# Attention: the queries' turn moved from a head's first step to its third, and their copy from ScalarE to VectorE

## What is computed

```python
Q, K, V = proj(Wq, bq), proj(Wk, bk), proj(Wv, bv)      # 64 heads x 2048 x 32
query_norms = jnp.linalg.norm(Q, axis=2)
_, top_idx = jax.lax.top_k(query_norms, top_u)          # top_u = 409
Q_sel = jnp.take_along_axis(Q, top_idx[:, :, None], axis=1)
scores = jnp.einsum('bud,bld->bul', Q_sel, K) * scale
attn = jax.nn.softmax(scores, axis=-1)
out_sel = jnp.einsum('bul,bld->bud', attn, V)
out_full = out_full.at[jnp.arange(BH)[:, None], top_idx].set(out_sel)
```

## Time and profile before

| | |
|---|---|
| median of 3 runs | 3328.67 us (3326.76 to 3335.19) |
| the profiled execution | 3315.01 us, span 3313.1 us |
| mean granted TensorE clock in it | 0.991 of full speed |
| TensorE busy | 95% |
| VectorE busy | 77% |
| GpSimd busy | 47% |
| ScalarE busy | 34% |

### The profile page before, as it was taken

How to read it: one execution, slowest core, us unless ns; L and a number is a source line. 1 busy time by engine, 2 the same in 40 slices (tenths; PEclk the granted TensorE clock), 3 DMA queues, 4 the chain that set the end, 5 groups by cost and what they waited for, 6 DMA issues and landing times.

```text
span 3313.1 us, 49640 instructions
## 1 busy us (share of the span) xinstructions
PE 3157.8 (95%) x16552; PEld 1456.3 (44%) x16552; DVE 2549.9 (77%) x3750; ACT 1141.7 (34%) x1588; POOL 1563.1 (47%) x1420
## 2 busy tenths in 40 slices
PE   7999999899999999999999999999999999999998
PEld 3543453333333333333355555555555555555554
DVE  4658967466666666666598998899898899998995
ACT  6853333365555555555411111111111111111111
POOL 3532225355656556554544444444444444444442
PEclk9999999899999999999999999999999999999999
DMA  6858859664333233223300001000110100011000
GB/s 233 284 174 248 232 138 247 173 193 118 77 101 101 79 99 105 72 76 94 92 26 29 29 32 32 32 28 28 32 32 28 32 28 28 32 32 31 30 19 16
DMA packets 238230, 290.81 MB, mean 88 GB/s; under 512 B 94648, under 2 KB 150328, under 8 KB 237384
## 3 DMA queue, kind: packets, MB, share of 16 engines
q1 hardware_dynamic: 221768, 283.07, 28.8%
q0 software_dynamic: 16384, 6.76, 1.1%
HBM read 169.36 MB, written 111.70 MB: 85 GB/s over the span
## 4 chain that ended last, share of the span: by engine, by line
PE 72%; ACT 3%; DVE 2%; issue 2%; POOL 1%; DMA 0%; SPq 0%; another core or an unknown queue 0%; ACTq 0%; POOLq 0%; DVEq 0%
PE bank L1624 10%; PE pair L2157 9%; PE pair L2158 9%; PE pair L2159 9%; PE pair L1613 7%; PE pair L1575 4%; PE bank L2180 4%; PE bank L2181 4%; PE bank L2179 4%; ACT shared L1516 3%; PE pair L2136 2%; PE pair L2138 2%; PE pair L2137 2%; PE bank L2169 1%; PE pair L2169 1%
## 5 line engine op out<-in xcount | busy, mean ns | idle before, releaser
L1411 DVE TENSOR_REDUCE top<-pair 128x1 f32<-128x1024 f32 x378 | 451.9, 1221 | 244.8 <-PE pair L1575 203.1
L1516 ACT ACTIVATE shared<-pair,p_bias 128x820 f32<-128x820 f32 x512 | 483.6, 945 | 425.5 <-PE pair L1613 337.4
L2157 PE MATMUL pair<-gu,xT_hi 128*128 128x512 f16 (+1 forms) x1536 | 555.0, 361 | 4.1 <-DVE bridge L1918 2.2
L2159 PE MATMUL pair<-gu,xT_lo 128*128 128x512 f16 (+1 forms) x1536 | 555.0, 361 | 0.0
L2158 PE MATMUL pair<-gu,xT_hi 128*128 128x512 f16 (+1 forms) x1536 | 555.0, 361 | 0.0
L1624 PE MATMUL bank<-shared,bridge 128*33 128x410 f32 x2048 | 406.0, 517 | 0.0
L1613 PE MATMUL pair<-q_exp,bridge 98*128 98x410 f16 x1024 | 268.1, 344 | 48.8 <-ACT shared L1516 45.4
L455 POOL DMA_INDIRECT q_sel<-q_d,chosen x256 | 246.2, 962 | 91.5 <-issue 76.1
L1372 POOL DMA_INDIRECT o_d<-o_rows,chosen x256 | 250.2, 977 | 81.5 <-issue 64.1
L2179 PE MATMUL bank<-dn,bridge 128*128 128x512 f16 x704 | 267.8, 380 | 0.0
L2180 PE MATMUL bank<-dn,bridge 128*128 128x512 f16 x704 | 267.8, 380 | 0.0
(11 more groups left out here) (270 smaller groups left out, 5999.6 us busy)
## 6 DMA issues: line engine op xcount, KB each, us to landing
bridge<-k_d SPq DMA_DIRECT2D x384, 128.0 KB
v_d<-v SPq DMA_DIRECT2D x16, 1056.0 KB
bridge<-v_d SPq DMA_DIRECT2D x64, 264.0 KB
x<-in_x SPq DMA_DIRECT2D x16, 1024.0 KB, 8.8
q_d<-q SPq DMA_DIRECT2D x16, 1024.0 KB, 4.3
a_in<-o_d SPq DMA_DIRECT2D x64, 256.0 KB, 2.6
f_x<-in_x SPq DMA_DIRECT2D x64, 256.0 KB, 2.6
out<-shared SPq DMA_DIRECT2D x64, 256.0 KB, 2.0
```

What stands on the lines that cost most here:

```text
L1411: ve.tensor_reduce(top[:, t, half:half + 1], ps[:, :, :].rearrange("p a n -> p (a n)"), AX.X, ALU.max, negate=True).then_inc(max_done, 1)
L1516: act.activation(p32[k % PB][:, :, :], ps_exp[:, :, 0:NQ], ACT.Exp, bias=con["p_bias"][:, 0:1], scale=scale).then_inc(p_done, 1)
L2157: pe.matmul(o, xT_hi[:, c, :], w_hi[:, c, c0:c0 + n], start=c == 0, stop=False)
L2159: last = pe.matmul(o, xT_lo[:, c, :], w_hi[:, c, c0:c0 + n], start=False, stop=c == KC - 1)
```

## The change

`turn_queries` of head i + 2 is placed at step 2 behind the chunks of that step, where it stood at step 0 ahead of them (`QUERIES_AT`). `take_queries` moves from ScalarE, where it stood behind the exponential of step 0, to VectorE, where it comes at step 2 behind `queries_again`. The computation is the same: the activation with Copy becomes a tensor_copy of the same 96 x 410 values.

```diff
-    QUERIES_AT = 0
+    QUERIES_AT = 2
...
+                def take_queries(h, u):
+                    ve.wait_ge(q_turned, h + 1)
+                    need(ve, max_ready, h * CH - CH)
+                    need(ve, qexp_done, h - 1)
+                    ve.tensor_copy(q_max[u][:, :], ps_misc[0:KROWS, 0:NQ]).then_inc(qsel_done, 1)
...
                 def first():
+                    ve.sem_inc(qsel_done, 2)
...
                         if k == OUT_AT and has(i, 1):
                             queries_again(i + 1, 1 - u)
+                        if k == QUERIES_AT and has(i, 2):
+                            take_queries(i + 2, u)
...
-                def take_queries(h, u):
-                    act.wait_ge(q_turned, h + 1)
-                    need(act, max_ready, h * CH - CH)
-                    need(act, qexp_done, h - 1)
-                    act.activation(q_max[u][:, :], ps_misc[0:KROWS, 0:NQ], ACT.Copy).then_inc(qsel_done, 1)
...
                 def first():
-                    act.sem_inc(qsel_done, 2)
...
                         exponentials(i, k)
-                        if k == QUERIES_AT and has(i, 2):
-                            take_queries(i + 2, u)
...
-                        if k == QUERIES_AT and has(i, 2):
-                            turn_queries(i + 2, u)
                         if k == GATHER_AT and has(i, 1):
                             gather_last(i + 1)
...
                                 scores_for_max(i + d, (u + d) % 2, c, in_turn(i, u, d))
+                        if k == QUERIES_AT and has(i, 2):
+                            turn_queries(i + 2, u)
```

## The result

The changed kernel took 3344.56 us (median of 7 runs, 3339.12 to 3346.41), the kernel before 3329.63 beside it (7 runs, 3326.76 to 3335.19). The ratio is 1.0037, 95% interval 1.0027 to 1.0047: slower, and just beyond the 0.3% within which I had put the likeliest case (3331 us). The profiled execution took 3344.4 us for a span of 3342.6. Every ratio in this document leaves out disturbed runs, of which there were two (8091 and 9274 us, both of the kernel before, beside experiments 5 to 8).

What follows compares the result with a forecast made beforehand. TensorE, busy 95% of the span, bounds the kernel. Turn 0 and ScalarE's copy 0, VectorE's late copy 2.3 us less 0.3 in unrolled heads: +2 us on 3328.7, so 3331 median (3317 profiled), range 3310 to 3350.

Steps and rivals of the forecast that it cites:

- the likeliest case: Whole kernel: within 10 us of before, 3331 us as median, chance 0.49.
- my sum: Attention heads: 19 heads at 0.12 us late, 2.3 us, less 0.3 in the unrolled heads: +2 us.
- the turn's hold on TensorE: Step 2, behind the chunks: the turn's four matmuls hold the array like one chunk matmul, 0.22 us, so nothing is lost.
- scores of step 5 that are late in a third of the heads: Where queries_again is long, 30% or 19 heads, VectorE's later copy makes TensorE's step 5 scores 0.12 us late.
- the loop's head would stay at 15.3 us: Loop of 56 heads: time per head unchanged at 15.3 us, against 14.26 in unrolled heads.
- my faster rival: ScalarE's late second exponential goes with the turn: 27 us at most, half taken, to 3315; chance 0.20 together with luck.
- some eight heads change sort: Luck in the loop: eight heads gain or lose a late second exponential, 1.2 us each, some 9 us either way.
- the crowd at step 0: Queries' turn, chunks and scores together in step 0, perhaps causing the second exponential's 31 waits of 1.2 us mean.
- The slower rival: VectorE's copy ends 0.2 to 0.3 us later, delaying TensorE's chunk in every head: 17 us, 3346; chance 0.31.
- the lead: TensorE's sequencer passes the wait for the queries 0.7 us ahead of the gather; the copy on VectorE loses this.
- the two signs by which I would know to be wrong: ScalarE's waits beside L1624 go away (faster), or scores of step 5 are late in nearly every head (slower).
- theory C1: From the experiments' forecasts: the loop's jump back to code that must be brought in again makes signals late.

Runs made afterwards that it cites:

- experiments 5 to 8: One chip: changed kernel written out, 0.9988; kernel before as single-round loops, 0.9988, and with eight slots a round, 1.0003; changed kernel with two-row transfers, 1.0001.
- experiment 2: Kernel before with only the queries' copy moved to VectorE behind queries_again, the turn left at step 0: 3305.22 us, ratio 0.9978 to the kernel before.
- Experiment 3: Changed kernel with VectorE's copy of the queries placed ahead of queries_again: 3334.75 us, ratio 1.0065 to the kernel before.
- experiment 10: Changed kernel with GpSimd's gathers of heads 8 to 59 and scatters of heads 1 to 53 cut to two rows per transfer: 3411.18 us, ratio 1.0363.
- experiment 9: Changed kernel unaltered, on a third chip: 3298.53 us against 3290.25 for the kernel before, ratio 1.0021.
- experiment 6: Kernel before with its 28 rounds as 28 single-round loops; register values were folded into constants, so it was written out: 3254.82 us, ratio 0.9988.
- experiment 4: Kernel before with its loop of 56 slots written out: 3266.58 us, ratio 0.9862 to the kernel before.
- experiment 7: Kernel before with a loop of 7 rounds of eight slots instead of 28 rounds of two: 3259.90 us, ratio 1.0003.

## Why the prediction was right and wrong

**The copy was right, the turn's price only in its total.** The copy on VectorE takes 0.58 us (predicted 0.57) and starts 0.28 us behind `queries_again`, as predicted. The chunk comes 0.33 us behind the gather in the head shown and 0.29 at the median of the loop's heads, where it came 0.16; I had 0.13 more. The turn's place: an undisturbed head goes from 14.23 to 14.26 us, 62 x 0.03 = 1.9 us, where my sum said +2. That agreement is luck, since it is made up otherwise: of a first step 0.07 us shorter, where I had put the gain at nothing, and a third 0.09 longer, where I had put the turn's hold on TensorE at 0.22 us and it is 0.44 (1044.04 to 1044.48); and not of scores of step 5 that are late in a third of the heads. The Trainium skill (VectorE: DVE Perf Modes, Specifications) says that ScalarE sits closer to PSUM. The rows agree, with 0.58 us on VectorE against 0.50 on ScalarE; as experiment 2 shows, that stands off the path.

**The step that failed** is "the loop's head would stay at 15.3 us". I had seen that about 1.04 us a head were lost in the loop for a reason I didn't know, and gave the change only two ways to touch it: the second exponential's waits might go (my faster rival, up to 27 us), or some eight heads change sort (9 us either way). The faster rival's premise came true: the second exponential is late in no head. But the loss wasn't tied to the crowd at step 0. It moved to between the fourth and the fifth exponential: over 2.3 us there in 43 heads against 19. The head did not stay: 47 heads of the loop take 15.40 us on average, which is nearly the 15.3, and nine take 17.4, because TensorE's clock fell in them. My sum had no term for a loss that moves with the order, and none for the clock.

**The slower rival had the sign and nearly the size (17 us against 15), for a wrong reason.** Its price was a late copy. Experiment 3 gave the lead back and was no faster for it; experiment 2 kept the late copy and was faster. Neither of the two signs by which I would know to be wrong told it: ScalarE's waits beside L1624 fell only from 36.2 to 22.4 us, and the scores of step 5 are late in hardly any head. That 3344.56 us lies in my range of 3310 to 3350 is therefore luck: the range reached so far up for this rival alone.

**How the loss holds itself**, argued from rows and not tested. In the head shown, the signals come at 1048.2. Behind them stand L1423, the output's turn and the divisions, until GpSimd starts L1364 at 1051.23 (3.0 us); GpSimd's scatters, cuts and gathers take it to 1062.69 (11.5 us); the signals of the next head come 1.1 us later, at 1063.8. That is a ring of 15.6 us, just the length of most of this loop's heads (15.58 here). Where signals don't wait for the gathers the ring isn't closed, and a head takes 14.3. Against this as the whole story: in experiment 10 GpSimd's gathers were shorter (0.87 us against 0.96 in the mean) and heads were longer, and before the change most late signals don't follow a fourth gather at this distance.

**The larger loss of the profiled execution is the clock.** In nine loop heads TensorE was granted 1.2 in place of 2.4 GHz for 3.4 us each. These heads take 17.2 to 17.9 us, 17.4 on average. Against the 15.30 of before they hold 18.6 of the loop's 23.4 us; the other 47, at 15.40, hold the rest. Windows of one such place:

```profile
1346.00:1349.50 3.50, 2.45 (x15) 0.85 (x12) 1.78 (x7) 0.96 (x2) 0.89 (x1) 1.00 0.28 75
1349.50:1352.90 3.40, 3.40 (x10) 0.57 (x8) 1.58 (x5) 0.94 (x1) 0.45 (x1) 0.50 0.00 0
1352.90:1356.00 3.10, 3.10 (x20) 1.21 (x20) 1.63 (x2) 2.29 (x3) 2.01 (x2) 1.00 0.02 5
```

The stretch ahead of it holds a late signal, with TensorE busy 2.45 of 3.5 us. The exponential inside comes 3.34 us behind the one ahead of it where 1.95 is usual. A head with a late fifth exponential and the full clock takes 15.6 us, so the half clock alone costs some 1.8 us in each of the nine, an estimate of 16 us in all. The two losses are tied, as far as the rows go: each of the nine heads also has a late signal, but 35 other heads have a late fifth exponential and no fall. Why the clock falls behind some late signals and not behind others is not shown.

The loop before has its clock at 1.00, the loop after at 0.98; in experiment 2's loop it is 1.00, in experiment 3's 0.99. Whole executions tell the same: the seven of the changed kernel have mean clocks of 0.984 to 0.988, and the two at 3339 us the highest of them; in experiment 9 the clock stays at 0.989 to 0.991, and the change costs 8 us in place of 15. The split into 18.6 and the rest is that of two profiles, not of the medians: the profile of before is of an execution faster than the median, and what a median one lost in its loop is not recorded.

**Still open:** what in a loop makes TensorE's signals late (the jump back to code already run, or waits by register, which experiment 6 was to tell apart and didn't), what chips without late signals have otherwise, and why smaller transfers make it worse. That code is loaded again at each jump back, which theory C1 supposed, is not seen. The queues that carry instructions, 720 to 1500 us, in the kernel before:

```profile
q14 instruction: 9, 0.07, 0.0%
q8 instruction: 1, 0.02, 0.0%
```

These are 10 packets for some 25 rounds; the kernel written out (experiment 4) moved 35 packets on q8 and 26 on q14 in the same window, and is faster.

## What to carry to other kernels

Compare the same piece of code inside and outside its loop before you cost a change in it. Where they differ by more than the change is worth, a sum of instructions doesn't forecast it; here it was 1.04 us a head against a change worth 0.03, and the thing to try first was the loop itself, written out (0.9% to 1.4% for the kernel before on chips with late signals, 0.1% on the one without). And ask of a loss of unknown cause not only whether it goes, but where it would turn up next. Count heads by their granted clock before you average them: nine heads of 56 held most of this loss.

## What the runs showed of the hardware

- The kernel before took 3259, 3288, 3290, 3312 and 3330 us in five sets of runs, each on one chip and steady within some 0.5%. Between the fastest chip (experiment 7, eight slots a round) and the slowest (the kernel before) the profiled spans differ by 57.8 us, of which the 56 loop heads have 54.8: 14.32 us a head, with no late signal, against 15.30.
- Written out, the heads took 14.23 to 14.43 us on each of the three chips tried.
- A loop costs 0.09 us a head even where nothing is late (14.32 against 14.23).
- In nine loop heads of the changed kernel the granted clock was 0.50 for 3.4 us, and they took 17.4 us in place of the 15.6 of heads with a late signal alone.
- Transfers of 2 rows in place of up to 128 made the loop's heads 17.2 us instead of 15.07 on one chip (16.2 in those with the full clock); on another the heads took 14.34 us, beside 14.32 for the kernel before with eight slots a round.
